# A fused tower on one core: GpSimd's masks ahead of its small jobs, and expert round one of five pairs placed behind the last attention

## What is computed

```python
h = einsum('bg,egp->bep', x, weight * mask) + bias      # weight 16 x 5000 x 128: 41 MB
h = h + attention(layernorm(h))                          # low-rank q and kv, rope, softmax
z = layernorm(h)
scores = sigmoid(z @ gate_w.T); top2, weights            # 64 experts
h = h + sum over the two of (silu(z @ w1[e]) * (z @ w3[e])) @ w2[e] * weight
      + (silu(z @ sw1) * (z @ sw3)) @ sw2                # the shared layer
```

## Time and profile before

| | us |
|---|---|
| median of 3 runs | 300.82 |
| lowest, highest | 298.55, 301.51 |
| the profiled execution: its time | 299.42 |
| its span, first to last instruction | 297.6 |
| busy: PE, DVE, POOL, ACT | 192.9, 174.6, 153.0, 74.5 |

### The profile page before, as it was taken

The page is one execution under the profiler, slowest core; times in us unless marked ns, Lnnn a source line. Parts: engine busy times, 40 slices in busy tenths (PEclk is TensorE's granted clock), DMA queues, the critical chain, the costliest instruction groups (busy, mean ns, idle before and its releaser), DMA issues.

```text
span 297.6 us, 5487 instructions
## 1 busy us (share of the span) xinstructions
PE 192.9 (65%) x2186; PEld 158.9 (53%) x2186; DVE 174.6 (59%) x435; ACT 74.5 (25%) x190; POOL 153.0 (51%) x120
## 2 busy tenths in 40 slices
PE   0089405979886978859948954664577589885020
PEld 0079305968675867757836842432366478763020
DVE  0034249776885687797797595577195433660072
ACT  2042000031412212312211212321259426341120
POOL 3256387097969667695694663250072220037540
PEclk9999965999995797985996985575579769999655
DMA  8999999999996688767996007956000207433223
GB/s 288 225 417 387 422 424 351 416 416 417 419 395 243 254 304 304 283 247 246 224 217 128 2 19 157 250 178 166 0 18 4 69 18 197 121 87 89 79 64 80
DMA packets 32867, 64.16 MB, mean 216 GB/s; under 512 B 2858, under 2 KB 25351, under 8 KB 32391
## 3 DMA queue, kind: packets, MB, share of 16 engines
q1 hardware_dynamic: 31384, 59.47, 60.3%
q0 software_dynamic: 1024, 2.10, 2.4%
q10 hardware_dynamic: 432, 2.21, 2.0%
HBM read 55.91 MB, written 7.86 MB: 214 GB/s over the span
## 4 chain that ended last, share of the span: by engine, by line
PE 33%; DVE 23%; SPq 15%; POOL 8%; issue 6%; DMA 5%; ACT 4%; another core or an unknown queue 3%; POOLq 1%; DVEq 0%
PE bank L702 10%; SPq L318 5%; DMA ring<-in_L_tok_weight_dram 4%; POOL ring L412 3%; PE bank L846 3%; PE bank L871 3%; DVE bank L1083 3%; POOL expert_inputs L432 3%; DVE ring L1029 3%; DVE bank L1062 2%; SPq L334 2%; DVE prod L1058 2%; DVE prod L1080 2%; PE bank L856 2%
## 5 line engine op out<-in xcount | busy, mean ns | idle before, releaser
L412 POOL TENSOR_TENSOR ring<-ring,mask 128x896 f32<-128x896 f32 (+1 forms) x48 | 92.5, 1948 | 22.5 <-DMA ring<-in_L_tok_weight_dram 22.4
L702 PE MATMUL bank<-ring,xT 128*64 128x128 f32 x1248 | 90.3, 305 | 19.4 <-POOL ring L412 16.9
L702 PEld LDWEIGHTS bank<-ring,xT 128*64 128x64 f32 x1248 | 80.0, 155 | 26.3 <-POOL ring L412 18.6
L1029 DVE TENSOR_TENSOR ring<-ring,bank 128x1024 f32<-128x1024 f32 (+1 forms) x45 | 46.3, 1047 | 35.7 <-DMA ring<-in_L_tok_weight_dram 35.5
L432 POOL DMA_INDIRECT expert_inputs<-xf,scatter_index x16 | 19.3, 1207 | 34.3 <-DVE scatter_index L1130 31.8
L401 POOL TENSOR_TENSOR rstd<-mv,half 128x1 f32<-128x1 f32 (+1 forms) x24 | 14.6, 607 | 41.9 <-DVE mv L1040 41.6
L481 POOL DMA_INDIRECT ring<-expert_outputs,gather_index x16 | 16.1, 1004 | 30.0 <-DMA expert_outputs<-ring 25.7
L1194 DVE TENSOR_TENSOR mask<-ring,bank 32x256 f32<-32x256 f32 (+1 forms) x24 | 10.0, 418 | 12.4 <-ACT ring L608 12.2
L1083 DVE TENSOR_REDUCE bank<-prod 128x128 f32<-128x256 f32 (+7 forms) x8 | 16.5, 2068 | 0.0
L515 ACT ACTIVATE offset<-shift,rstd 128x1 f32<-128x1 f32 x16 | 4.7, 295 | 46.2 <-POOL rstd L401 46.2
L846 PE MATMUL bank<-w,ring 128*64 128x128 f32 (+1 forms) x256 | 14.8, 296 | 1.6 <-DVE ring L1185 1.5
(11 more groups left out here) (142 smaller groups left out, 307.9 us busy)
## 6 DMA issues: line engine op xcount, KB each, us to landing
ring<-in_L_tok_weight_dram SPq DMA_DIRECT2D x48, 832.0 KB, 9.9
ring<-expert_inputs SPq DMA_DIRECT2D x6, 512.0 KB, 5.9
expert_outputs<-ring SPq DMA_DIRECT2D x12, 256.0 KB, 2.3
mask<-in_L_tok_mask_dram SPq DMA_DIRECT2D x3, 832.0 KB, 15.3
expert_inputs<-prod ACTq DMA_DIRECT2D x2, 1024.0 KB, 12.2
w2p<-in_L_ffn_w_dram SPq DMA_DIRECT2D x2, 1024.0 KB, 10.7
w<-in_x_dram SPq DMA_DIRECT2D x1, 1250.0 KB, 12.7
expert_inputs<-ring SPq DMA_DIRECT2D x1, 1024.0 KB, 13.4
```

Of the source, the lines that this page charges most:

```text
L412: pool.tensor_tensor(unit(j, q, SPLIT(q // 2), UC), unit(j, q, SPLIT(q // 2), UC), mask[:, (m + SPLIT(q // 2)) * D:(m + UC) * D], ALU.mult ...
L702: last = pe.matmul(bank[0][64 * par:64 * par + 64, 0:D], xT[:, (UC * t + c) * B:(UC * t + c + 1) * B], unit(j, 2 * t + par, c, c + 1), sta ...
L1029: dve.tensor_tensor(both(j, t, a, b), both(j, t, a, b), m.rearrange("p (u f) -> p u f", u=1).to_broadcast([P, 2, (b - a) * D]), ALU.mult). ...
```

## The change

**GpSimd's share in the loop.** POOL now does three pieces, the roots of h2 and qk, three pieces, the root of h, and only then the scatter. DVE computes the statistics for that root (`stats_h`) ahead of `scores` instead of behind `less_max`.

**Rounds.** Round one has pairs 0 to 4 (`NCH1 = 5`), round two pairs 5 to 7. The slots of round two are zeroed in the loop (turn c = 1, on ACT's queue, from a tile of zeros) and no longer in the tail; `scores(0)` waits for that too. The weights of `down` are loaded right behind those of `up`, all but 16 rows that lie under the tokenizer's remainder.

**The tail.** The eight groups of round one are put between the steps of attention 5, 6 and 7, by hand, on all engines. All their products are POOL's. The two halves of the shared layer stand together behind group 7 and ahead of round two. ACT copies all turned inputs; the combine steps of pairs 0 to 4 stand between the products of round two on DVE; the routing weights are computed in two parts. Pair 6's attention uses bank 0 instead of bank 6 for its small results.

```diff
-NCH1 = 6
+NCH1 = 5
-POOL_SHARE = (2, 2, 2)
+POOL_SHARE = (3, 3)
...
 def T_BANK(g):
-    return (0, 2)[g % 2]
+    return 2 if g < GROUPS1 else (0, 2)[g % 2]
...
+def A_BANK(j):
+    return 0 if j == NCH - 2 else 6
...
@@ SP: loads
-            sp.wait_ge(s_zsrc, 2)
-            sp.dma_start(xs_dram[1].rearrange("(p r) d -> p (r d)", p=P), zeros).then_inc(s_zero[1], 16)
+            sp.wait_ge(s_tok, 3 * (NCH - 1))
             sp.wait_ge(s_scat[0], 16 * 2 * NCH1)
             for i in range(GROUPS1 // 2):
                 load_slots(0, i)
...
@@ POOL: the loop, then the tail
                 mask_pieces(POOL_SHARE[1])
+                if c >= 1:
+                    root_h(c - 1)
                 if d >= 0:
                     scatter(d)
-                mask_pieces(POOL_SHARE[2])
-                if c >= 1:
-                    root_h(c - 1)
...
+            root_h(NCH - 1)
+            root_qk(NCH - 2)
             root_h2(NCH - 3)
-            root_qk(NCH - 2)
-            root_h(NCH - 1)
+            mid(0)
+            root_qk(NCH - 1)
             scatter(NCH - 3)
...
+            mid(1)
+            mid(2)
+            mid(3)
             root_h2(NCH - 2)
+            mid(4)
+            mid(5)
+            mid(6)
+            root_h2(NCH - 1)
+            mid(7)
             scatter(NCH - 2)
...
@@ ACT: turn c = 1
+                    act.dma_start(xs_dram[1].rearrange("(p r) d -> p (r d)", p=P), prod[:, 0:2048]).then_inc(s_zero[1], 16)
...
@@ PE: behind the sums (j, k, l = 5, 6, 7), middle and end of the new list
+            turn_mid(4)
+            down(3)
+            turn_xs(7)
+            up(6)
+            turn_mid(5)
+            down(4)
             turn_o(l)
             attend(l)
+            rank_tokens(k)
+            up(7)
+            turn_mid(6)
+            down(5)
             turn_xf(l)
             gate(l)
+            turn_mid(7)
+            down(6)
             rank_tokens(l)
-            expert_steps(STEPS_C, GROUPS1)
+            down(7)
+            shared(0)
+            shared(1)
...
@@ DVE: turn of the loop
                 if d >= 0:
                     place(d)
+                if a >= 0:
+                    stats_h(a)
                 if b >= 0:
                     scores(b)
                 mask_pieces(VECTOR_SHARE[4])
                 if b >= 0:
                     less_max(b)
-                if a >= 0:
-                    stats_h(a)
...
@@ DVE: the tail
             heads(k)
-            norm_qk(l)
+            scores(l)
+            less_max(l)
             add_attended(k)
+            heads(l)
             choose(k)
             place(k)
-            add_shared(0)
-            scores(l)
-            less_max(l)
-            heads(l)
             add_attended(l)
             choose(l)
             place(l)
             gather_slots(1, NCH1, NCH)
-            dve.wait_ge(s_hmz, 4)
-            dve.wait_ge(s_hm, STEPS_C)
-            for g in range(STEPS_C, GROUPS1):
-                mid(g)
-
+            shared_mid(0)
+            add_shared(0)
+            shared_mid(1)
+            add_shared(1)
...
+            combine(0)
             for g in range(GROUPS1, GROUPS):
                 mid(g)
-                if g + 2 < GROUPS:
-                    copy_xsT(g + 2)
...
+                combine(1 + g - GROUPS1)
```

More of the change, by code:

```diff
@@ L368, in _ @@
                 load_slots(1, i)
-            for g in range(STORED_EARLY, GROUPS):
+            for g in range(GROUPS1, GROUPS):
                 store_group(g)
@@ new lines, in silu_shared, with score_exp @@
+                act.activation(ssil, bank[1][:], ACT.Silu).then_inc(s_ssil, 1)
+            def score_exp(first, last):
+                act.wait_ge(s_top, last)
+                act.activation(ew[:, 0, first:last], top[:, first:last, 0:2], ACT.Exp, scale=-1.0).then_inc(s_exp, 1)
+            j, k, l = NCH - 3, NCH - 2, NCH - 1
+            keep_h(l)
+            copy_xnT(k)
+            copy_oT(j)
+            score_exp(0, NCH1)
+            norm_xf(j)
+            turned_qk(k)
+            copy_xfT(j)
@@ new lines, in _ @@
+            norm_h(l)
+            copy_xsT(0)
+            heads_k(k)
+            heads_v(k)
+            copy_xsT(1)
+            copy_xnT(l)
+            silu(0)
+            copy_xsT(2)
+            probs(k)
+            copy_midT(0)
+            copy_xsT(3)
+            turned_qk(l)
+            silu(1)
+            heads_k(l)
+            heads_v(l)
+            silu(2)
+            copy_oT(k)
+            copy_midT(1)
+            copy_y(0)
+            copy_xsT(4)
+            silu(3)
@@ new lines, in _ @@
+            copy_midT(2)
+            copy_y(1)
+            copy_xsT(5)
+            probs(l)
+            norm_xf(k)
+            copy_midT(3)
+            copy_y(2)
+            copy_xsT(6)
+            copy_xfT(k)
+            silu(4)
+            copy_midT(4)
+            copy_y(3)
+            copy_xsT(7)
+            silu(5)
+            copy_midT(5)
+            copy_y(4)
+            silu(6)
+            copy_oT(l)
+            copy_midT(6)
+            copy_y(5)
+            norm_xf(l)
@@ L942, in _ @@
             last.then_inc(s_total, 1)
-            expert_steps(GROUPS1, GROUPS + 2)
-            shared(1)
+            turn_xs(GROUPS1)
+            turn_xs(GROUPS1 + 1)
+            for g in range(GROUPS1, GROUPS + 2):
+                if g < GROUPS:
+                    up(g)
+                if GROUPS1 < g <= GROUPS:
+                    turn_mid(g - 1)
+                if g >= GROUPS1 + 2:
+                    down(g - 2)
+                if g + 2 < GROUPS:
+                    turn_xs(g + 2)
             full = pe.value_load(flag_i[0:1, 0:1], min_val=0, max_val=1)
@@ L1105, in add_attended @@
                 dve.wait_ge(s_att, j + 1)
[L1106 removed]
+                then(dve.tensor_tensor(hres[:, j, :], hres[:, j, :], bank[A_BANK(j)][:, P:P + D], ALU.add))
                 then(dve.bn_stats(stats[:, 3, :], hres[:, j, :]))
@@ L1242, in combine @@
                                          ALU.mult, ALU.add).then_inc(s_fin, 1)
-            dve.wait_ge(s_xsT, GROUPS1)
-            copy_xsT(GROUPS1)
-            copy_xsT(GROUPS1 + 1)
+            j, k, l = NCH - 3, NCH - 2, NCH - 1
+            dve.wait_ge(s_xn, l)
+            stats_h(l)
+            stats_qk(k)
+            add_attended(j)
+            norm_qk(k)
+            gather_slots(0, 0, NCH1)
+            weights(0, NCH1)
+            choose(j)
+            scores(k)
+            less_max(k)
@@ new lines, in _ @@
+            stats_qk(l)
+            place(j)
+            norm_qk(l)
+            heads(k)
+            scores(l)
+            less_max(l)
+            add_attended(k)
+            heads(l)
+            choose(k)
+            place(k)
+            add_attended(l)
+            choose(l)
+            place(l)
+            gather_slots(1, NCH1, NCH)
+            shared_mid(0)
+            add_shared(0)
+            shared_mid(1)
+            add_shared(1)
+            dve.wait_ge(s_total, 1)
+            for r in range(2):
+                mark(dve.tensor_reduce(flag[:, r:r + 1], bank[6][:, E * r:E * r + E], AX.X, ALU.max))
@@ L1260, in _ @@
-            marked()
-            add_shared(1)
-            for j in range(NCH):
+                combine(1 + g - GROUPS1)
+            weights(NCH1, NCH)
+            for j in range(NCH1, NCH):
                 combine(j)
```

295 lines of the change are left out of this document (138 added, 157 removed).

## The result

| | before | after |
|---|---|---|
| median, us | 300.82 | 291.27 |
| lowest, highest | 298.55, 301.51 | 289.89, 292.96 |
| profiled execution, its span | 299.42, 297.6 | 292.96, 291.2 |

The account below looks back on a forecast made before the run. No engine is full; a ladder of small steps handed between engines sets the end. Pair 7 placed at 240.5 plus 46.3 us to the end gives a span of 286.8, with 1.8 around it 288.6 us; range 280 to 298.

Parts of the forecast that it names:

- POOL's third piece ahead of the scatter takes away what c = 3 loses: Loop, turn c = 3: DVE's idle time for `attend` falls from 4.62 to 1.69 us, a gain of 2.9 us.
- the early `stats_h` costs nothing net: Loop, DVE: some 0.8 us of work moves ahead of the scores and covers the wait for the values; net zero.
- in c = 4 to 7 the DVE ladder decides, and there I count nothing: Loop, later turns: DVE's chain of attention steps sets the pace, so no gain was counted.
- the +2.0: Loop, turn 2: more zeros cost 2.8 us of stream; less half of `stats_h`'s 1.2 us, DVE's start shifts +2.0 us.
- Attention 6 and 7: Behind the sums: `o` of 7 at 221.2 instead of 232.85, turn held behind `down(4)` until 228.0, pair 7 placed at 240.5.
- The shared layer: Slots to round two: two halves of 5.3 to 7.4 us each, ending 11.2 to 15.4 behind the slots; 12.5 taken.
- Round two and landing: Tail behind the shared layer: round two from an empty pipeline, with store 0.4 and landing 2.3, takes 18.4 us.
- The first: Rival, tail: PE's results come late while POOL gathers, steps stretch by some 6 us; 294.6 us, chance 0.20.
- The second: Rival, round one: groups follow at PE's full rate, output of 7 turned at once, placed at 234.5; 282.6 us, chance 0.14.
- The third: Rival, round one: groups hold up attention, each of six costing 1.6 us more, pair 7 placed at 250; 298 us, chance 0.08.
- The fourth: Rival, whole tail: PE stays at the lower clock, mean near 0.5 from 183 to the slots; 306.6 us, chance 0.08.
- The table switch: ACT behind the sums: six switches counted at 1.28 us each; by the skill's 2.66 the sum would be up to 5.5 longer.

Follow-up runs that it names:

- e2: Changed kernel with the loop's part undone (POOL's pieces 2, 2, 2 with the scatter between, statistics of h behind `less_max`): 300.23 us, ratio 0.998.
- e10: Kernel before with POOL's three pieces, two roots, three pieces, then scatter and root of h; statistics of h not moved: 301.92 us, ratio 1.003.
- e1: Kernel before with the loop's part alone: POOL's pieces and root of h ahead of the scatter, statistics of h ahead of the scores: 294.58 us, ratio 0.977.
- e12: Changed kernel with useless matmuls where PE stands idle, from attention 7 to the end of the shared layer: 289.53 us, ratio 0.965.
- e7: Changed kernel with the shared layer's second half behind round two and combines behind round two's products: 281.85 us, ratio 0.955, on the chip of 295.2.
- e3: Changed kernel with the output writes held until the last stores of round two have landed: 292.77 us, ratio 0.970.
- e9: Kernel before with round one's gathers held until all groups are copied: 300.33 us, ratio 1.002.
- e6: Changed kernel with the end of attention 7 taken ahead on all four engines, `o(7)` turned behind `turn_mid(4)`: 282.33 us, ratio 0.957, on the chip of 295.2.
- e8: e7 with the earlier turn of `o(7)` of e6: 274.83 us, ratio 0.932, on the chip of 295.2.
- e13: e8 with both shared halves behind round two and round two's load ahead of round one's last two stores: 284.51 us, ratio 0.944, chip of 299.9.
- e4: Changed kernel with combines behind round two's products and gathers held until the shared layer is added: executions too far apart for a ratio, profiled one 287.67 us.

## Why the prediction was right, and where it was not

The time (291.27 for 288.6), the sign and the range held, in good part by luck. In spans, I had 1.0 us from the loop and 9.8 behind the turn of o(5); the profile has 4.1 and 2.3 (117.5 us from there to the end before, 115.1 after), and e2 says that the second part alone is worth nothing. A gain that I hadn't counted stood in for most of one that didn't come. The rest is that the medians lie 9.5 us apart and the two profiles only 6.5, and where those 3 us are, no trace shows.

- **The loop, the step that failed.** Three statements failed: "POOL's third piece ahead of the scatter takes away what c = 3 loses", "the early `stats_h` costs nothing net", and "in c = 4 to 7 the DVE ladder decides, and there I count nothing". e10 has the third piece without the early statistics: PE's wait for POOL is gone there too, o(1) is turned no earlier and nothing is gained. With both, e1 turns o(1) 3.5 us and o(5) 5.7 us earlier than before, so 2.2 come in c = 4 to 7. The turn at 93.5, as forecast, hid this: it is -3.5 and some 2.4 for the zeros. I had priced the early statistics by the work they move on DVE (0.8 us) and not by who waits for them: the root of h, and behind it on POOL the next turn's pieces. The zeros, with the other new loads, cost 1.6 to 2.0 at o(5), as the +2.0 said; -2.9 + 2.0 should have been -5.7 + 1.6.
- **Attention 6 and 7.** From the turn of o(5) to `o` of 7: 40.4 us, forecast 42.1. The turn then held for 7.7 (forecast 6.8), and turn to slots 13.6 (12.5). Slots at 237.9 for 240.5, the difference being the loop's.
- **The shared layer, mis-sized.** Slots to the first turn took 16.8 us, where I took 12.5 from bounds of 11.2 to 15.4. The last copy of round one ended 2.1 us behind the slots and not 0.6. And I had read the 3.02 us of the earlier trace rows as the price at the lower clock; the clock rose within that row (granted 0.50 from 193.8 to 196, 0.92 from 196 to 197), and wholly at the lower level the same four matmuls take 3.75. Both halves ran them so. e12 shows why: PE was busy 5.72 of the 10 us from 228 on, the clock fell at 232.1 and came back only at 252.6; with PE kept busy it stayed. e7 shows that the fall need not meet the layer. I had the lower clock as a rival for the whole tail; it came in one stretch, mostly behind the slots.
- **Round two and landing.** First turn to last copy 17.3 for 15.7, of which 2 us are the late signal at 257.27. Last copy to first gather 5.0 for 3.5; e3 shows that this is not the output writes. Gathers and sums 9.8 for 10.2, output 4.4 as forecast. The tail's sum is 53.3 for 46.3: 7.0 too long, against 2.6 gained ahead.
- **The rivals.** The first (late results under gathers) is real and its price moved: 12 us in the kernel before (e9), 2 in the changed one, whose gathers run out just as round two starts, 6 as soon as the shared layer is quick (e12). By my own sign of being wrong (copies that wait for ended matmuls while POOL gathers) it was there. The second, the turn of `o(7)` at once, is not what this order does; e6 does it, with slots at 226.3 and a ratio of 0.957. The third didn't happen: from the turn of o(5) to the slots it took 61.8 us, forecast 61.4. The fourth was off by its own test (mean clock 0.78 from 183 to 238 us) and came true only for the shared layer.
- **The table switch.** Behind the sums every load is again 1.28 us with the next activation 1.3 us behind its start (208.38, 209.68). The row was the right one to go by. The further 1.38 us of the Trainium skill, page "ScalarE: Activation LUTs", section "What ACT_TABLE_LOAD costs", are not in this trace: the copy ahead of that load ended at 208.36.

## What to carry to other kernels

Price a step that is moved by who waits for its result and what stands in line behind that waiter, not by its own length: 0.8 us of statistics, moved ahead of a long step together with a root and two pieces, was worth more than a rewritten tail, though the two pieces without the statistics and the root were worth nothing. When independent work is woven into a ladder of small steps, look at both ends, at the ladder's ready results that stand in line, and at the engine that idles between its steps; on one chip, turning one result earlier took the ratio from 0.955 to 0.932 (e7 to e8), and half of the shared layer under the landing of the stores took it from 0.957 to the same 0.932 (e6 to e8). A clock level that one profile shows in one stretch is not yet the work of the edit. Measure the parts of a change one by one even when the sum comes out as forecast.

## What was not expected of the hardware

- GpSimd's indirect gathers can slow TensorE's issue: three to five matmuls each 1.4 us (e13), results late by 5.8 us (e12), last copy 12 us later (e10 against e9). It showed in profiles from two of three chips. In those of e4, e6, e7 and e8, all from the chip where the kernel before is 5 us faster, the same gathers ran beside round two with no late result; one `up` of e7 took 1.93 us, at a granted clock of 0.50. What makes the difference, and what gathers and TensorE share, is open.
- Adding 27 matmuls of no use to TensorE's list made the shared layer 4 us shorter, by the clock (granted 1.00 for 0.71 in the 10 us ahead of it, and 1.00 for 0.50 under its first matmuls).
- Taking waits of one engine away (PE for POOL, in e10) can leave the time as it was: they came back in full as waits for another (DVE).
